# Target-order scatters of edge rows: where GpSimd waits for their landing

## What is computed

```python
edge_index = jnp.stack([src, dst])
x = x + _L0_gnn_ref(_layernorm(x), edge_index, ...)
x = x + _L0_ffn_ref(_layernorm(x)[None], ...)[0]
...                                    # _L1_gnn_ref, with edge_attr = edge_attr_256:
e = (edge_attr @ We).reshape(-1, H, C)
k_j = k[src] + e
v_j = v[src] + e
q_i = q[dst]
alpha = jnp.sum(q_i * k_j, axis=-1) / jnp.sqrt(jnp.float32(C))
...                                    # softmax of alpha over the edges of a dst
out = jax.ops.segment_sum(v_j * alpha[:, :, None], dst, num_segments=n)
```

## Time and profile before

| | |
|---|---|
| median of 3 runs | 5103.01 us |
| profiled execution: its own time, its span | 5104.09 us, 5102.3 us |
| TensorE busy | 3706.8 us (73%) |
| VectorE busy | 2898.2 us (57%) |
| ScalarE busy | 1658.3 us (33%) |
| GpSimd busy | 2644.4 us (52%) |
| scatters into `by_dst` (L1447) | 416, mean 999 ns, 415.4 us busy, 261.9 us idle before them |
| loads of `dst_row` | 52 of 1024 KB |

### The profile page before, as it was taken

The page is one execution under the profiler, slowest core; times in us unless marked ns, Lnnn a source line. Parts: engine busy times, 40 slices in busy tenths (PEclk is TensorE's granted clock), DMA queues, the critical chain, the costliest instruction groups (busy, mean ns, idle before and its releaser), DMA issues. The chain is left out here.

```text
span 5102.3 us, 75134 instructions
## 1 busy us (share of the span) xinstructions
PE 3706.8 (73%) x20786; PEld 2965.0 (58%) x20786; DVE 2898.2 (57%) x5915; ACT 1658.3 (33%) x3757; POOL 2644.4 (52%) x2597
## 2 busy tenths in 40 slices
PE   7883539476898999813608999848999858777178
PEld 6662327365777777602406888726777646666065
DVE  8783528056787888743127898724333545554553
ACT  5562213101333333201205766523333313333033
POOL 0055645566777777557576777630000067776400
PEclk6586659788999999855759999977999967887579
DMA  5044444458999999723417888711000046776300
GB/s 75 9 161 145 120 142 140 145 182 268 294 307 299 300 309 302 229 79 94 128 48 203 244 242 238 212 51 59 0 0 0 23 135 192 198 199 190 110 13 25
DMA packets 642022, 779.41 MB, mean 153 GB/s; under 512 B 149190, under 2 KB 562361, under 8 KB 638106
## 3 DMA queue, kind: packets, MB, share of 16 engines
q0 software_dynamic: 120624, 316.61, 20.6%
q1 hardware_dynamic: 350852, 284.27, 19.8%
q10 hardware_dynamic: 170374, 176.38, 11.0%
HBM read 509.08 MB, written 272.20 MB: 153 GB/s over the span
## 5 line engine op out<-in xcount | busy, mean ns | idle before, releaser
L2018 POOL DMA_INDIRECT a_far<-kv_table,a_index x416 | 486.0, 1168 | 146.0 <-issue 118.3
L1447 POOL DMA_INDIRECT by_dst<-dst_row,place x416 | 415.4, 999 | 261.9 <-issue 121.0
L2599 POOL DMA_INDIRECT fl_far<-x_table,fl_index x416 | 453.3, 1090 | 143.9 <-issue 126.5
L2333 POOL DMA_INDIRECT a_far<-src_table,a_index x416 | 452.9, 1089 | 132.1 <-issue 123.1
L2636 PE MATMUL ps<-fl_w,fl_hid 128*128 128x256 f32 x1664 | 398.8, 382 | 20.1 <-ACT ps L2708 19.0
L2052 PE MATMUL ps<-a_w,a_edge_t 128*128 128x256 f32 x1664 | 407.1, 389 | 0.0
L3304 POOL DMA_INDIRECT starts<-p_near,p_at x25 | 24.3, 974 | 709.2 <-DMA starts<-p_zero 694.1
L2636 PEld LDWEIGHTS ps<-fl_w,fl_hid 128*128 128x128 f32 x1664 | 309.5, 191 | 66.4 <-issue 27.5
L2188 DVE TENSOR_TENSOR a_far<-ps,a_far 128x1024 f32<-128x1024 f32 x208 | 253.9, 1220 | 164.9 <-PE ps L2052 148.0
L2052 PEld LDWEIGHTS ps<-a_w,a_edge_t 128*128 128x128 f32 x1664 | 311.4, 197 | 36.1
L1078 ACT ACTIVATE f_hid<-ps,f_bn 128x320 f32<-128x320 f32 x320 | 197.6, 617 | 328.6 <-PE ps L1032 328.6
(11 more groups left out here) (535 smaller groups left out, 9476.9 us busy)
## 6 DMA issues: line engine op xcount, KB each, us to landing
partial<-a_out ACTq DMA_DIRECT2D x208, 546.0 KB, 4.6
a_edge<-by_dst SPq DMA_DIRECT2D x104, 516.0 KB, 6.4
partial_f<-fl_out ACTq DMA_DIRECT2D x26, 2056.0 KB
dst_row<-in_edge_attr SPq DMA_DIRECT2D x52, 1024.0 KB, 5.9
xn_sb<-q_table SPq DMA_DIRECT2D x416, 128.0 KB
fl_keys<-key_rows SPq DMA_DIRECT2D x26, 1024.0 KB, 5.3
a_keys<-local_rows SPq DMA_DIRECT2D x104, 128.0 KB
xt<-partial SPq DMA_DIRECT2D x14, 512.0 KB, 4.9
```

The source lines that it names most:

```text
L1447: self.nc.gpsimd.indirect_dma_start(out=self.table, out_offset=bass.IndirectOffsetOnAxis(ap=self.place[:, n:n + 1], axis=0), in_=self.row[ ...
L2018: gathered[b % 4].count(nc.gpsimd.indirect_dma_start(out=far[:, b, u, :], out_offset=None, in_=kv_table, in_offset=bass.IndirectOffsetOnAx ...
L2333: gathered[b].count(nc.gpsimd.indirect_dma_start(out=far[:, b, u, :], out_offset=None, in_=src_table, in_offset=bass.IndirectOffsetOnAxis( ...
L2599: gathered[q * 4 + t // 4].count(nc.gpsimd.indirect_dma_start(out=far[:, q, t, :], out_offset=None, in_=table, in_offset=bass.IndirectOffs ...
```

## The change

GpSimd no longer waits behind each four scatters for the landing of these four. In place of it, it waits once in an item, ahead of the fifth scatter and behind the join of the next item, until the item in front has landed. The first item of a share does not wait at all. Narrow rows and shares with `between` have neither wait, as before.

```diff
     def scatter(self, pool, j, first, between=None):
-        k, uses = self.ring(j)
+        k = self.ring(j)[0]
         if j == self.looped:
             self.join(pool, j)
         pool.wait_ge(self.joined, (j + 1) * (2 if self.narrow else 1) + 2 * self.looped)
...
                 self.join(pool, j + 1)
             if t % 4 == 0 and between is not None:
                 between(2 * (j - first) + t // 4)
+            if t == 4 and j > first and not self.narrow and between is None:
+                before, uses = self.ring(j - 1)
+                pool.wait_ge(self.scattered[before], (uses + 1) * self.TILES_AN_ITEM * 16)
             n = self.first_tile(j) + t
             self.nc.gpsimd.indirect_dma_start(out=self.table, out_offset=bass.IndirectOffsetOnAxis(ap=self.place[:, n:n + 1], axis=0),
                                               in_=self.row[:, k, t, :], in_offset=None,
                                               bounds_check=EPAD - 1, oob_is_err=False).then_inc(self.scattered[k], 16)
-            if t % 4 == 3 and not self.narrow and between is None:
-                pool.wait_ge(self.scattered[k], (uses * self.TILES_AN_ITEM + t + 1) * 16)
```

## The result

| | kernel before | changed kernel |
|---|---|---|
| median, us (four runs each) | 5101.85 | 4914.69 |
| lowest to highest | 5096.69 to 5126.44 | 4906.60 to 4924.55 |
| profiled execution, its own time | 5104.09 | 4906.60 |
| its span | 5102.3 | 4904.8 |

The ratio is 0.9633 (95% interval 0.9607 to 0.9659): 187 us faster by the medians. The forecast was 160 us, 4943, with a range down to 4925. The direction and the mechanism held; the gain is larger than the range allowed. The changed kernel was timed again on a second chip, with the same result (ratio 0.9642), and on two more in a variant with smaller row loads (0.9653 and 0.9631). On a further chip it is 3.4% slower than the kernel before, and on one more each part of the change is slower by itself; that is the second half of this text.

What follows compares the result with a forecast made beforehand. The prediction took GpSimd's scatter issue with its two landing waits an item to bound the target-order scatter stages. Savings of 66.2 + 3.0 + 22 + 69.3 = 160.5 us from 5104.1 gave 4943; range 4925 to 5000.

Steps and rivals of the forecast that it cites:

- What bounds the stages: Target-order scatter stages: GpSimd and its landing waits come last; without them VectorE ends place and f0, GpSimd still g0.
- The pace: GpSimd without the two waits: an item of eight scatters takes 10.3 us against 14.8, read from project stage p1.
- The new wait is free: Mid-item wait for the item in front: costed at 0, with 2.8 us of cover; at most 2.3 us an item.
- Place, 66.2: Place stage, 17 items: 66.2 us saved, capped by VectorE ending last at 435.6; bounds 44 and 66.
- n0, 3.0: Stage behind place, one item: normed_table stores start earlier, 3.0 us saved; bounds 0 and 3.
- g0, 22: Stage of 6 items behind fifty gathers, GpSimd last before and after: 22 us saved; bounds 8 and 24.5.
- f0, 69.3: First feed-forward, 20 items: 69.3 us saved, capped by VectorE's last operation at 956.6; lower bound 42.
- the way out and in costs 6.2 us, which I keep: End of place: from SyncE's last load to the next stage's first scatter, 6.2 us, taken as unchanged.
- the landing once an item: Rival: scatters land slower than 5.1 us, so GpSimd pays one landing an item, 12.6 us: 5007 us; chance 0.10.
- VectorE slowed in place: Rival: denser scatter issue holds VectorE in the place stage, which ends 46 us later: 4989 us; chance 0.06.
- late row loads: Rival: undrained scatters delay SyncE's row loads, GpSimd stands at the join: 5242 us if loads take 45 us; chance 0.03.
- slower: Outcome above the kernel before, by row loads coming late beside undrained scatters: 5242 us at 45 us a load; chance 0.03.

Runs made afterwards that it cites:

- f0 alone: Kernel before with the new wait only in the first feed-forward's 20 items, old waits elsewhere: 5036.25 us, 0.9847 on chip 1; 5844.57 us, 1.019 on chip 7.
- no_wait: Changed kernel without its own new wait: 5948.41 us, ratio 1.0369 on chip 7; 4932.34 us, 0.9643 on chip 10.
- own_once: Kernel before with one wait an item in every stage, behind the eighth scatter for all eight, in place of two: 5748.42 us, ratio 1.0007 on chip 12.
- the mixed version: Kernel before with one wait an item in f0, and the new rule only in the last items of place and f0: ratios 0.9866, 0.9865, 0.9879.

## Why the forecast was right in kind and short in size

- **What bounds the stages** held: with the waits gone, place and f0 end with VectorE, g0 with GpSimd.
- **The pace** held: 10.3 us an item, as read from p1.
- **The new wait is free** held, shown by the pair with and without it on chip 10.
- **Place, 66.2**: measured 70.8. 2.6 us are the way out, 2.0 us VectorE ending at 433.6 in place of 435.6. **n0, 3.0**: 3.6.
- **g0, 22**: measured 27.9. The deduction of 2.5 us for stretched scatters was wrong in sign: the mean fell from 1100 to 1037 ns. Issuing takes 65.3 us of the stage, 26.4 less. The other 1.5 us contradict "the landing at the end stays": GpSimd no longer waits for the last landing before its DRAIN, whose 8.1 us now follow the last scatter directly.
- **f0, 69.3**: 74.2 in the first pair, 74.7 with f0 alone. All but 0.1 us of the difference is the way out.
- **The sum up to a1** is 177.0 against 160.5. The step that failed is the sentence "the way out and in costs 6.2 us, which I keep" and its silent twin in f0. GpSimd's DRAIN was part of that price and is paid only where GpSimd comes last: from the last load or the last VectorE operation to the next stage's first, 5.4 us became 2.8 behind place, and 6.3 became 1.5 behind f0. Of the 16.5 us missed, 8.9 are the ends of the three stages (2.6, 4.8 and g0's 1.5), 4.4 the scatters of g0, 2.0 VectorE's end, and about 1 in n0, n2 and p1. The range's lower end named this ("room for the exit barriers being cheaper") and gave it too little.
- **The rest of the median's 187**, 10 us, is not located and need not be of the change: the interval is 13 us to either side, the stages behind p1 spread by 40 us between executions, and the unedited place by up to 16 (n0 reached at 507.2, 513.3 and 523.3). The stage gains alone, 177, would have given 4925 from the median of 5101.85, the very edge of the range; what took the median below it is in this open part.
- **The rivals**: the landing once an item, VectorE slowed in place (place ended 2 us earlier, not 46 later) and late row loads are excluded on the ordinary chips. The page that the prediction set against itself (the Trainium skill, SBUF — State Buffer, "SBUF: two separate sides") has VectorE in a two-port mode and GpSimd lock each other out of shared ports. In g0 single scatters beside VectorE's work were still stretched, to 2.17 us at most, which agrees with it; but the mean got shorter, and VectorE in place was not slowed.
- **What no rival had**: on chip 12 the change costs 3.4%, and on chip 7 its parts cost 3.5% together. I gave "slower" 0.03, by another mechanism. The profile of before could not show this one, since none of its rows has a late signal.

**Open.** Why two of the chips behave so is not settled, nor whether it belongs to the chip or to the time of its one visit, nor whether recording the execution has a part in it. Nothing in these profiles names a path that is full: in f0 on chips 1 and 7 the rates and shares are alike at first. Shown are the place (stages with indirect DMAs, not all of them), the trigger (the removed waits, stage by stage) and the form (engines held with no releaser). Whether the trigger is the pace of the scatters or their number in flight is open, since each edit moves both; a kernel that holds the pace and bounds the number in flight was not tried. The new wait's own bound does not help: no_wait on chip 7 and the changed kernel on chip 12 reach n0 at 595.0 and 595.4. Whether the row loads take part was to be told by the kernel with 64 B loads, and whether the mixed version wins there by the mixed kernel; neither met such a chip.

## What to carry to other kernels

Where a wait is removed and another engine becomes the last of a stage, also count what the old last engine did after its work: its DRAIN leaves the path with it. A wait for landings may also be a throttle: before it is removed, time the kernel on more than one chip, and look for idle time with no releaser. If one version must serve all chips, one wait an item in f0 is the only edit here that gained in its stage on both kinds (45 us, and 48 as part of own_once), though by itself it was not timed on a slow chip. On ordinary chips no version that writes the right rows was faster than the change as made.

## What the runs showed of the hardware

- GpSimd's DRAIN ends 3.3 us behind the last scatter or its awaited landing in place, 8.1 in g0 and 5.3 in f0, the same in both kernels. Where no wait holds the sequencer its record starts while scatters are still to be made (9.4, 14.3 and 11.8 us long), so the length of the record is not the price.
- The same program (the kernel before) takes 12.4 to 12.7% longer on chips 7 and 12 than on 5, 10 and 1; on chip 12 all but 4 us of it lie in six stages with indirect DMAs. The new rule in f0 alone is 1.9% slower on chip 7 and 1.5% faster on chip 1.
- Row loads of 1 MB an item beside dense scatters cost nothing measurable on the ordinary chips: 34.3% of the DMA engines' time or 0.8% in f0, ratios of 0.9642 and 0.9639 on the same chip.
